# Attention and feed-forward layer: value products by head pair over 512 queries, three buffers of transposed probabilities, output blocks of two pairs

## The chip, the cores and the metric

The kernel runs on one core of one Trainium2 chip. The metric is the device time of one execution in microseconds, as the median of the runs shown. A profile is one further execution with its own time.

## The reference, cut to what matters

All tensors are float32: `x` is (8, 512, 256), there are 16 heads of 64, and the feed-forward part has 1024 hidden columns.

```python
def attn(x, gamma, w_qkv, w_out):            # called on layernorm(x)
    xn = rms_norm(x, gamma)
    q, k, v = split_heads(xn @ w_qkv)        # each (8, 16, 512, 64)
    sim = (q * 64**-0.5) @ k.transpose
    out = softmax(sim) @ v                   # (8, 16, 512, 64)
    return merge_heads(out) @ w_out

x = x + attn(layernorm(x), gamma, w_qkv, w_out)
x = x + ffn(layernorm(x), router_w, w1, b1, w2, b2)
# ffn: gelu(x @ w1 + b1) @ w2 + b2, times the sum of the two normalised top router weights
```

## The kernel before, in words

Every large product is computed from operands split in a high and a low fp32r part. The projections, the scores and the output projection take three products per tile (high·high, low·high, high·low, `products`, line 551); the products with the values take the high and the low part of the transposed probabilities against one set of values (`weighted_values`, line 617), whose high and low parts stand side by side in 128 stationary columns.

The attention is a pipeline of steps written out by hand. A head pair has four tiles n of 128 queries, so the 64 pairs give 256 tiles (`NUNIT`), and a step handles two: step s computes the scores of tiles 2s and 2s+1, and transposes the probabilities of tiles 2s-3 and 2s-2. Each engine runs its own list of work in a fixed order (the loops at lines 779, 914, 1020 and 1249), and semaphores join the lists. TensorE in step s does, in this order: transposes of tile 2s-3 into PSUM banks 4 and 5, scores of 2s and 2s+1 (banks 0 to 3), transposes of 2s-2 into banks 6 and 7, the auxiliary blocks of place 1, the products with the values of half t = s-2 (256 queries, both heads, bank 5), and the other auxiliary blocks.

An auxiliary block is one PSUM bank of other work: the query and key projections of the next pair (`q` in bank 4 and `k` in bank 6, on even steps), value projections of four heads (`v`, bank 4, on odd steps), and a tile of the output projection (`out`, bank 6, on odd steps). `plan_aux` (line 82) decides which block goes to which step and place; the place gives the bank (`PS_AUX`). An `out` block sums four pairs for one tile of 128 tokens (256 columns), and VectorE adds it to the residual `xres` (`aux_done`, line 1112); to keep four pairs and more, the attention output has `NATT` = 7 buffers.

The banks 4 to 7 are used in turn by transposes, by auxiliary blocks and by the value products, so a transpose waits until VectorE and ScalarE have emptied what stood there (`transpose_prob`, line 587). VectorE in step s does: reciprocal of the row sums of 2s-1 (L1189), the late auxiliary blocks of step s-1 (place above 1, among them `k` and `out`), low part of the transposed tile 2s-3 in two instructions (L1100), row maximum of 2s (L1184), low part of 2s-2, row maximum of 2s+1, reciprocal for 2s, the auxiliary blocks of place 1 (`q` or `v`), and last the layer norm work of a later input. ScalarE makes the high parts (L875 and L872), the exponentials (L882) and the copy of the value products to `halves_out` (L892). SyncE regroups that copy by DMA (`regroup`, line 439), and GpSimd normalises the probabilities (L974) and adds and splits the regrouped output (`attention_out`, line 1003).

The feed-forward part follows over eight inputs; its first products (`up`) lie in the last two attention steps, and its hidden values reuse the buffers `pT`.

Of the kernel before, what the change touches and what calls it, by code (L numbers as in the profile page):

```python
# [27 lines left out]
ALU = mybir.AluOpType  # L28
# [41 lines left out]
PS_OUT = 5  # L70
PS_AUX = {1: 4, 2: 6, 3: 7, 4: 5, 5: 4, 6: 5}
# [10 lines left out]
def plan_aux():  # L82
# [3 lines left out]
    for step in range(FIRST_STEP, LAST_STEP + 1):  # L86
        blocks = []
        if step == -4:
            blocks += [(2, "xt", 0), (3, "xt", 1)]
        if step == -3:  # L90
            blocks += [(1, "k", 0), (2, "q", 0)]
        if step == 0:
            blocks += [(5, "v", 0, 0), (6, "v", 0, 1)]
        if step % 2 == 0 and step // 2 + 1 in range(1, NPAIR):
            blocks += [(1, "q", step // 2 + 1), (2 if step else 4, "k", step // 2 + 1)]
        place = 2 if step < 11 else 1
        if step % 4 == 3 and (step + 1) // 4 in range(1, NPAIR // 2):
            blocks.append((place, "v", (step + 1) // 4, 0))
        if step % 4 == 1 and step // 4 in range(1, NPAIR // 2):
            blocks.append((place, "v", step // 4, 1))  # L100
# [11 lines left out]
    for tile in range(TT):  # L112
        task = ("out", 2 * B - 1, tile)
        index[task] = len(index)
        last_out.append((index[task], 0, *task))
# [3 lines left out]
def layer_kernel(nc, x, gamma_cols, w_qkv, w_out, router_w, w1, b1_cols, w2, b2_rows, ident, out):  # L119
# [11 lines left out]
    with ExitStack() as ctx:  # L131
# [39 lines left out]
        pT = [sb("pT_hi", [P, 2, 2 * TT, 2 * P], F32R), sb("pT_lo", [P, 2, 2 * TT, 2 * P], F32R)]  # L171
# [4 lines left out]
        halves_out = sb("halves_out", [P, 2, 2, 2 * P], F32, att)  # L176
# [17 lines left out]
        f_hT = [p[:, :, :, :].rearrange("p a k q -> p (a k q)").rearrange("p (f q) -> p f q", f=FT) for p in pT]  # L194
# [210 lines left out]
        def odd_tiles(n):  # L405

            t, u = divmod(n, 2)
            return [[p[:, t % 2, :, u * P + r * DH:u * P + (r + 1) * DH] for p in pT] for r in range(2)]

        def even_tile(n):  # L410
            t, u = divmod(n, 2)
            return [p[:, t % 2, :, u * P:(u + 1) * P].rearrange("p a (r q) -> p a r q", r=2) for p in pT]
# [12 lines left out]
        def _(sp):  # L425
# [13 lines left out]
            def regroup(pair):  # L439

                sp.wait_ge(s_halves, 2 * pair + 2)
                if pair >= 1:
                    sp.wait_ge(s_att, pair)
                for dst, rows, src_rows, h in ((att_hi_v, 0, 0, 0), (att_hi_v, DH, DH, 1),
                                               (att_lo_v, 0, DH, 0), (att_lo_v, DH, 0, 1)):
                    sp.dma_start(dst[rows:rows + DH, :].rearrange("p (a q) -> p a q", a=2),
                                 halves_out[src_rows:src_rows + DH, :, h, :]).then_inc(s_merge, 16)
# [23 lines left out]
            for slot in range(FIRST_SLOT, LAST_SLOT + 1):  # L471
# [21 lines left out]
                if rel == 19 and 1 <= b < B:  # L493
                    sp.wait_ge(s_aux, aux_index[("out", 2 * b - 1, TT - 1)] + 1)
                    sp.dma_start(x1_dram[b - 1], xres[:, :, :]).then_inc(s_x1, 16)
                if rel == 20 and 0 <= b < B:
                    if b >= 1:
                        sp.wait_ge(s_x1, 16 * b)
                    sp.dma_start(xres[:, :, :], x_v[b]).then_inc(s_xres, 16)
                    store_blocks(b + 1)  # L500
# [27 lines left out]
            sp.wait_ge(s_aux, aux_index[("out", 2 * B - 1, TT - 1)] + 1)  # L528
# [21 lines left out]
        def _(pe):  # L550
# [36 lines left out]
            def transpose_prob(n):  # L587
# [4 lines left out]
                before_rest = [block for block in before_rest if block[1] < 4]  # L592
                if n == 1:
                    pe.wait_ge(s_aux, aux_index[("v", 0, 1)] + 1)
                if n % 2:
# [21 lines left out]
            def weighted_values(t):  # L617

                pair = t // 2
                quad = pair // 2  # L620
                pe.wait_ge(s_ptlo, 4 * t + 4)
                pe.wait_ge(s_aux, aux_index[("v", quad, 1)] + 1)
                for h in range(2):
                    for part in range(2):
                        for k in range(TT):
                            ins = pe.matmul(ps[:, PS_OUT, h * 2 * P:(h + 1) * 2 * P],  # L626
                                            vbuf[:, quad % 2, k, pair % 2 * 2 + h, :],
                                            pT[part][:, t % 2, h * TT + k, :], start=part == 0 and k == 0,
                                            stop=part == 1 and k == TT - 1)
                ins.then_inc(s_pv, 1)  # L630
# [17 lines left out]
            def aux(step, block_no, place, kind, *args):  # L648

                tile = 2 * step - 3 if place == 1 else 2 * step - 2  # L650
                same_bank = [j + 1 for j in range(block_no) if aux_bank(j) == aux_bank(block_no)]
                if place and 0 <= tile < NUNIT:
# [42 lines left out]
                elif kind == "out":  # L695
                    half, tile = args
                    wait_weight_split(pe, 7)
                    for j in range(4):
                        pair = 4 * half + j
                        if tile == 0:  # L700
                            pe.wait_ge(s_att, pair + 1)
                        ins = products(bank[:, 0:D],
                                       [a[:, pair % NATT, tile * P:(tile + 1) * P] for a in attT],
                                       [w[:, pair % PAIRS, :] for w in wout], j == 0, j == 3)
# [3 lines left out]
            def last_outs():  # L708
# [6 lines left out]
                for j in range(4):  # L715
                    pair = NPAIR - 4 + j
                    pe.wait_ge(s_att, pair + 1)
                    for block_no, _, _, _, tile in last_out:
                        ins = products(ps[:, aux_bank(block_no), 0:D],
                                       [a[:, pair % NATT, tile * P:(tile + 1) * P] for a in attT],  # L720
                                       [w[:, pair % PAIRS, :] for w in wout], j == 0, j == 3)
                        if j == 3:
# [36 lines left out]
            def down(c, tile):  # L759
# [3 lines left out]
                for f in range(FT):  # L763
                    if tile == 0:
                        pe.wait_ge(s_hlo, c * FT + f + 1)
                    ins = products(ps[:, down_bank(c, tile), t * D:(t + 1) * D],
                                   [h[:, f, tile * P:(tile + 1) * P] for h in f_hT],
# [11 lines left out]
            for step in range(FIRST_STEP, LAST_STEP + 1):  # L779
# [16 lines left out]
                if 0 <= step - 2 < STEPS:  # L796
                    weighted_values(step - 2)
# [28 lines left out]
        def _(act):  # L826
# [39 lines left out]
            def transposed_hi(n):  # L866
                t = n // 2
                act.wait_ge(s_pt, 2 * n + 2)
                if n % 2 == 0:
                    if t >= 2:  # L870
                        act.wait_ge(s_pv, t - 1)
# [15 lines left out]
            def copy_halves(t):  # L887
                pair, part = divmod(t, 2)
                act.wait_ge(s_pv, t + 1)
                if part == 0 and pair >= 1:  # L890
                    act.wait_ge(s_merge, 64 * pair)
                act.activation(halves_out[:, part, :, :],  # L892
                               ps[:, PS_OUT, :].rearrange("p (h q) -> p h q", h=2), ACT.Copy).then_inc(s_halves, 1)
# [20 lines left out]
            for step in range(FIRST_STEP, LAST_STEP + 1):  # L914
# [5 lines left out]
                if step == 1:  # L920
                    exp(3)
                if 0 <= 2 * step - 3 < NUNIT:
# [12 lines left out]
                if 0 <= step - 2 < STEPS:  # L935
                    copy_halves(step - 2)
# [7 lines left out]


# [18 lines left out]
        def _(pool):  # L964
# [11 lines left out]
            def hidden_hi(n):  # L976
                c, f = divmod(n, FT)
                pool.wait_ge(s_gelu, n + 1)
                if c == 0 and f in (0, TT):
                    pool.wait_ge(s_pv, NHEAD - 1 + f // TT)  # L980
                if c >= 1 and f == 0:
                    pool.wait_ge(s_down, 2 * c)
                pool.tensor_scalar(f_hT[0][:, f, :], f_h[n % 3], 1.0, 1.0, ALU.mult, ALU.mult)\  # L983
# [19 lines left out]
            def attention_out(pair):  # L1003
# [3 lines left out]
                if pair >= NATT:  # L1007
                    pool.wait_ge(s_aux, aux_index[("out", (pair - NATT) // 4, TT - 1)] + 1)
# [400 lines left out]
```

## Time and profile before

| | |
|---|---|
| median of 3 runs | 1178.37 us (1178.27 to 1178.46) |
| the profiled execution's own time | 1178.86 us |
| its span, first to last instruction | 1177.0 us |
| TensorE matmul busy | 1164.9 us (99%) |
| VectorE busy | 977.3 us (83%) |
| ScalarE busy | 872.2 us (74%) |
| GpSimd busy | 665.6 us (57%) |

Busy time counts the instructions of an engine; TensorE's matmuls are pipelined, so that one matmul's span overlaps the next one's. The distance from one matmul's start to the next one's start is what it costs in a stream. In the timelines, PE is TensorE's matmul, PEld its weight load, DVE VectorE, ACT ScalarE, POOL GpSimd. The transposes of a tile (L612) begin a step: from one start of an odd tile's transposes to the next is the length of a step.

### The profile page before, as it was taken

How to read it: one execution, taken by the hardware profiler on the slowest of the kernel's cores; microseconds unless marked ns; L12 is line 12 of the kernel's file. 1: busy time of each engine (PE TensorE's matmuls, PEld its weight loads, DVE VectorE, ACT ScalarE, POOL GpSimd, SP SyncE). 2: the span in 40 equal slices, each digit the busy share in tenths (PEclk: the TensorE clock that was granted, in tenths of full speed). 3: DMA queues.
4: the chain of work that ended last, by engine and by line, in shares of the span. 5: the costliest groups of instructions: out<-in, count | busy, mean ns of one | idle time of the engine just before them, and what ended most of it. 6: DMA issues, size and time to landing. Idle time of an engine off the chain costs nothing.

```text
span 1177.0 us, 28904 instructions
## 1 busy us (share of the span) xinstructions
PE 1164.9 (99%) x11195; PEld 1024.8 (87%) x11195; DVE 977.3 (83%) x1736; ACT 872.2 (74%) x1897; POOL 665.6 (57%) x826
## 2 busy tenths in 40 slices
PE   8999999999999999999999999999999999999999
PEld 6778888888888888888888888888888887998898
DVE  6888888888888888889888988898889888877764
ACT  6888888888888888888888888888888885334432
POOL 5776565655556655656565656565656576223321
PEclk9999999999999999999999999999999999999999
DMA  4234111411141114111421132113211335334321
GB/s 125 61 88 109 33 32 33 123 37 38 37 127 37 38 37 126 37 38 37 117 47 37 38 92 69 33 33 85 72 38 37 91 90 150 127 111 145 109 74 36
DMA packets 74663, 83.08 MB, mean 71 GB/s; under 512 B 12576, under 2 KB 67360, under 8 KB 74528
## 3 DMA queue, kind: packets, MB, share of 16 engines
q1 hardware_dynamic: 74528, 81.24, 25.8%
q8 instruction: 89, 1.46, 0.5%
q14 instruction: 46, 0.38, 0.1%
HBM read 31.14 MB, written 16.25 MB: 40 GB/s over the span
## 4 chain that ended last, share of the span: by engine, by line
PE 86%; POOL 4%; DVE 2%; issue 2%; ACT 2%; POOLq 0%; DVEq 0%; ACTq 0%
PE ps L555 43%; PE ps L626 18%; PE ps L612 11%; PE ps L578 9%; PE ps L584 4%; POOL prob L974 1%; DVE pT_lo L1100 1%; ACT prob L882 1%; DVE negmax L1184 1%; POOL att_hi_v L1005 1%; POOL attT_lo L1011 1%; PE ps L741 1%; POOL wout_lo L995 0%; POOL attT_hi L974 0%; POOL wbig_lo L995 0%
## 5 line engine op out<-in xcount | busy, mean ns | idle before, releaser
L974 POOL TENSOR_SCALAR prob<-prob,rowinv 128x512 f32<-128x512 f32 x512 | 353.1, 704 | 241.5 <-DVE rowinv L1189 240.3
L882 ACT ACTIVATE prob<-ps,negmax 128x512 f32<-128x512 f32 x512 | 346.6, 685 | 34.6 <-DVE negmax L1184 30.6
L1100 DVE TENSOR_TENSOR pT_lo<-ps,pT_hi 128x512 fp32r<-128x512 f32 (+1 forms) x384 | 319.8, 860 | 19.9 <-ACT pT_hi L875 14.9
L1184 DVE TENSOR_REDUCE negmax<-ps 128x2 f32<-128x1024 f32 x256 | 310.2, 1212 | 1.4 <-PE ps L584 1.4
L872 ACT ACTIVATE pT_hi<-ps 128x1024 fp32r<-128x1024 f32 x128 | 131.4, 1027 | 101.1 <-issue 100.4
L612 PEld LDWEIGHTS ps<-identity,prob 64*128 64x128 f32 x4096 | 154.8, 138 | 58.2 <-issue 20.4
L612 PE MATMUL ps<-identity,prob 64*128 64x64 f32 x4096 | 177.9, 226 | 2.5 <-DVE vbuf L1100 1.1
L578 PE MATMUL ps<-nat 64*128 64x512 f32 x1024 | 171.0, 411 | 0.3 <-DVE nat L1101 0.3
L626 PE MATMUL ps<-pT_hi,vbuf 128*128 128x256 f32 x1024 | 164.7, 283 | 1.3 <-DVE pT_lo L1100 1.2
L626 PE MATMUL ps<-pT_lo,vbuf 128*128 128x256 f32 x1024 | 164.5, 283 | 0.0
L626 PEld LDWEIGHTS ps<-pT_hi,vbuf 128*128 128x128 f32 x1024 | 145.0, 191 | 7.4 <-DVE pT_lo L1100 2.0
L875 ACT ACTIVATE pT_hi<-ps 128x512 fp32r<-128x512 f32 x256 | 140.1, 608 | 10.4 <-PE ps L612 10.4
L626 PEld LDWEIGHTS ps<-pT_lo,vbuf 128*128 128x128 f32 x1024 | 141.2, 192 | 0.0
L1005 POOL TENSOR_TENSOR att_hi_v<-att_hi_v,att_lo_v 128x512 f32<-128x512 f32 x64 | 83.4, 1303 | 97.3 <-DMA att_lo_v<-halves_out 97.3
L555 PE MATMUL ps<-xT_hi,wbig_hi 128*128 128x512 f32 x316 | 131.4, 416 | 0.1
L555 PE MATMUL ps<-xT_hi,wbig_lo 128*128 128x512 f32 x316 | 124.5, 394 | 0.0
L555 PE MATMUL ps<-xT_lo,wbig_hi 128*128 128x512 f32 x316 | 123.0, 389 | 0.0
L1189 DVE RECIPROCAL rowinv<-rowsum 128x2 f32<-128x2 f32 x256 | 40.6, 159 | 92.9 <-ACT prob L882 92.6
L882 ACT ACTIVATION_READ_ACCUMULATOR prob<-ps,negmax 128x1 f32 x512 | 102.7, 201 | 0.0
L983 POOL TENSOR_SCALAR pT_hi<-prob 128x512 fp32r<-128x512 f32 x64 | 50.6, 795 | 90.8 <-ACT prob L899 90.8
L584 PE MATMUL ps<-nat 64*128 64x512 f32 x512 | 101.7, 394 | 0.0
L578 PEld LDWEIGHTS ps<-nat 64*128 64x128 f32 x1024 | 87.4, 188 | 12.9 <-DVE nat L1101 0.7
(114 smaller groups left out, 2292.4 us busy)
## 6 DMA issues: line engine op xcount, KB each, us to landing
att_hi_v<-halves_out SPq DMA_DIRECT2D x128, 128.0 KB, 2.3
att_lo_v<-halves_out SPq DMA_DIRECT2D x128, 128.0 KB, 2.4
blocks_scratch<-xblocks SPq DMA_DIRECT2D x15, 512.0 KB, 5.1
xn<-blocks_scratch SPq DMA_DIRECT2D x60, 128.0 KB, 2.8
xin<-in_x SPq DMA_DIRECT2D x32, 128.0 KB, 3.2
xres<-in_x SPq DMA_DIRECT2D x8, 512.0 KB, 4.3
x_scratch<-xres SPq DMA_DIRECT2D x8, 512.0 KB, 3.6
xin<-x_scratch SPq DMA_DIRECT2D x32, 128.0 KB, 3.2
```

What stands on the lines that cost most here:

```text
L555: ins = pe.matmul(dst, stationary[i], moving[j], start=first and n == 0, stop=last and n == len(terms) - 1)
L578: pe.matmul(ps[:, PS_SCORE[n % 2] + h, :], part[rows, q_part, q0:q0 + P], part[rows, k_part, :], start=q_part == QH, stop=False)
L584: pe.matmul(ps[:, PS_SCORE[n % 2] + h, :], part[rows, QH, q0:q0 + P], part[rows, KL, :], start=False, stop=True).then_inc(s_score, 1)
L612: ins = pe.transpose(ps[:, bank + r, a * DH:(a + 1) * DH], prob[rows, n % NPROB, a * P:(a + 1) * P], identity[rows, rows])
L626: ins = pe.matmul(ps[:, PS_OUT, h * 2 * P:(h + 1) * 2 * P], vbuf[:, quad % 2, k, pair % 2 * 2 + h, :], pT[part][:, t % 2, h * TT + k, :], ...
L872: act.activation(even_tile(n)[0], two_bank_blocks(PS_PT_EVEN), ACT.Copy).then_inc(s_pthi, 2)
L875: act.activation(odd_tiles(n)[r][0], bank_blocks(PS_PT_ODD + r), ACT.Copy).then_inc(s_pthi, 1)
L882: act.activation(prob[:, n % NPROB, j * SEQ:(j + 1) * SEQ], ps[:, PS_SCORE[n % 2] + j, :], ACT.Exp, bias=negmax[:, n % 4, j:j + 1], accum_ ...
L974: return pool.tensor_scalar(dst, src, scalar, 1.0, ALU.mult, ALU.mult)
L1005: pool.tensor_tensor(att_hi_v[:, :], att_hi_v[:, :], att_lo_v[:, :], ALU.add).then_inc(s_head, 1)
L1100: return dve.tensor_tensor(dst, full, hi, ALU.subtract)
L1184: dve.tensor_reduce(negmax[:, n % 4, :], ps[:, PS_SCORE[n % 2]:PS_SCORE[n % 2] + 2, :], AX.X, ALU.max, negate=True).then_inc(s_max, 1)
```

## The change

The products with the values are issued once for a pair instead of once for half of its queries: on every odd step, each of the two heads gets its own bank (5 and 6) and a matmul has 512 moving columns. For this `pT` has three buffers of 256 queries. When a pair's two halves lie in buffers 2 and 0, the buffers are read in the order 0, 2, and the tokens of that pair are permuted (`pair_tokens`). An `out` block sums two pairs instead of four, for two tiles of 128 tokens (512 columns of a bank), on every even step, in bank 5; `attT` has three buffers instead of seven. `q`, `v` and `out` are now in the first group of a step (place 1 or 2), `k` alone is late (place 3, bank 6). ScalarE copies one head at a time: head 0 within the odd step, head 1 at the start of the next step. GpSimd's `attention_out` moves behind the normalisation of tile 2s. The copy of `xres` in and out of memory moves to earlier slots; the last output blocks sum two pairs instead of four, and VectorE adds them before the last two hidden values.

```diff
-PS_OUT = 5
-PS_AUX = {1: 4, 2: 6, 3: 7, 4: 5, 5: 4, 6: 5}
+PS_VALUES = (5, 6)
+PS_AUX = {1: 4, 2: 5, 3: 6, 4: 5, 5: 4, 6: 5, 7: 6, 8: 7}
@@ plan_aux
-            blocks += [(1, "q", step // 2 + 1), (2 if step else 4, "k", step // 2 + 1)]
-        place = 2 if step < 11 else 1
+            blocks += [(1, "q", step // 2 + 1), (3 if step else 4, "k", step // 2 + 1)]
...
-        for half in range(2 * B - 1):
-            since = step - (8 * half + 11)
-            steps = (0, 2, 3, 4) if half == 2 * B - 2 else (0, 2, 4, 6)
-            if since in steps:
-                blocks.append((2, "out", half, steps.index(since)))
+        for quarter in range(NPAIR // 2 - 1):
+            since = step - (4 * quarter + 8)
+            if quarter == NPAIR // 2 - 2 and since == 0:
+                blocks += [(1, "out", quarter, 0), (2, "out", quarter, 1)]
+            elif quarter < NPAIR // 2 - 2 and since in (0, 2):
+                blocks.append((2, "out", quarter, since // 2))
@@ buffers
+        NHALF = 3
+        pT = [sb("pT_hi", [P, NHALF, 2 * TT, 2 * P], F32R), sb("pT_lo", [P, NHALF, 2 * TT, 2 * P], F32R)]
-        NATT = 7
+        NATT = 3
@@ aux_of: which blocks of a step are first, which late
-            return [block for block in blocks if block[1] == 1], [block for block in blocks if block[1] > 1]
+            return [block for block in blocks if block[1] <= 2], [block for block in blocks if block[1] > 2]
+        def pair_at(step):
+            pair, odd = divmod(step - 3, 2)
+            return pair if not odd and 0 <= pair < NPAIR else None
@@ regroup
-                sp.wait_ge(s_halves, 2 * pair + 2)
...
+                for h, dst in ((0, (att_hi_v, att_lo_v)), (1, (att_lo_v, att_hi_v))):
+                    sp.wait_ge(s_halves, 2 * pair + h + 1)
...
@@ transpose_prob
+                valued = pair_at(step - 1)
                 if n % 2:
                     if before_first:
                         pe.wait_ge(s_aux, before_first[-1][0] + 1)
                     elif n >= 2:
                         pe.wait_ge(s_ptlo, 2 * (n - 2) + 2)
-                    if step >= 3:
-                        pe.wait_ge(s_halves, step - 2)
+                    if valued is not None:
+                        pe.wait_ge(s_halves, 2 * valued + 1)
                 else:
...
+                    if valued is not None:
+                        pe.wait_ge(s_halves, 2 * valued + 2)
@@ weighted_values
-                pe.wait_ge(s_ptlo, 4 * t + 4)
                 for h in range(2):
+                    pe.wait_ge(s_ptlo, 2 * min(TT * pair + TT + h, NUNIT))
                     for part in range(2):
                         for k in range(TT):
-                            ins = pe.matmul(ps[:, PS_OUT, h * 2 * P:(h + 1) * 2 * P], ...
-                                            pT[part][:, t % 2, h * TT + k, :], ...
+                            ins = pe.matmul(ps[:, PS_VALUES[h], :], ...
+                                            pT[part][:, halves_of(pair)[0], h * TT + k, :], ...
@@ aux, kind "out"
+                    quarter, part = args
+                    for i in range(2):
+                        for pair in (2 * quarter, 2 * quarter + 1):
+                            ins = products(bank[:, i * D:(i + 1) * D],
+                                           [a[:, pair % NATT, pair_tokens(pair, 2 * part + i)] for a in attT],
+                                           [w[:, pair % PAIRS, :] for w in wout], pair % 2 == 0, pair % 2 == 1)
@@ ScalarE's loop
+                if pair_at(step - 1) is not None:
+                    copy_halves(pair_at(step - 1), 1)
                 if 0 <= 2 * step - 3 < NUNIT:
                     transposed_hi(2 * step - 3)
...
-                if 0 <= step - 2 < STEPS:
-                    copy_halves(step - 2)
+                if pair_at(step) is not None and step < LAST_STEP:
+                    copy_halves(pair_at(step), 0)
@@ GpSimd's loop
-                if step % 2 == 0 and 0 <= step // 2 - 2 < NPAIR:
-                    attention_out(step // 2 - 2)
...
                     normalise_prob(2 * step)
+                if pair_at(step - 1) is not None:
+                    attention_out(pair_at(step - 1))
@@ VectorE, aux_done, kind "out"
-                    dve.tensor_tensor(xres[:, tile, :], bank[:, 0:D], xres[:, tile, :], ALU.add)\
-                        .then_inc(s_aux, 1)
+                    tiles = slice(2 * part, 2 * part + 2)
+                    dve.tensor_tensor(xres[:, tiles, :], bank.rearrange("p (t d) -> p t d", t=2), xres[:, tiles, :],
+                                      ALU.add).then_inc(s_aux, 1)
@@ VectorE, feed-forward loop, first input
+                    if f == FT - 3 and c == 0:
+                        for block_of_out in last_out:
+                            aux_done(*block_of_out)
                 if c == 0:
-                    for block_of_out in last_out:
-                        aux_done(*block_of_out)
```

## Rows read from the trace of the kernel before

**Rows 1.** The page: busy times, the clock in 40 slices.

```profile
PE 1164.9 (99%) x11195; PEld 1024.8 (87%) x11195; DVE 977.3 (83%) x1736; ACT 872.2 (74%) x1897; POOL 665.6 (57%) x826
...
PEclk9999999999999999999999999999999999999999
```

**Rows 2.** Timeline of TensorE, an even step: start, us, line, operation, tiles.

```profile
401.00 0.71 PE L612 MATMUL ps<-identity,prob 64*128 64x64 f32 x16
...
403.57 0.50 PE L555 MATMUL ps<-xT_hi,wbig_hi 128*128 128x512 f32 x1
...
405.07 0.64 PE L626 MATMUL ps<-pT_hi,vbuf 128*128 128x256 f32 x4
...
406.98 0.40 PE L555 MATMUL ps<-xT_hi,wbig_hi 128*128 128x512 f32 x1
...
408.14 0.39 PE L555 MATMUL ps<-xT_lo,wbig_hi 128*128 128x512 f32 x1
```

**Rows 3.** The same timeline, the odd step behind it.

```profile
408.46 0.71 PE L612 MATMUL ps<-identity,prob 64*128 64x64 f32 x16
...
412.59 0.64 PE L626 MATMUL ps<-pT_hi,vbuf 128*128 128x256 f32 x4
...
414.51 0.28 PE L555 MATMUL ps<-wout_hi,attT_hi 128*128 128x256 f32 x1
...
416.04 0.71 PE L612 MATMUL ps<-identity,prob 64*128 64x64 f32 x16
```

**Rows 4.** Timeline of VectorE in the even step.

```profile
402.41 1.29 DVE L1100 TENSOR_TENSOR pT_lo<-ps,pT_hi 128x512 fp32r<-128x512 f32 x2 [0.27 <-ACT pT_hi L875]
...
404.89 1.22 DVE L1100 TENSOR_TENSOR pT_lo<-ps,pT_hi 128x1024 fp32r<-128x1024 f32 x1
...
407.16 0.15 DVE L1189 RECIPROCAL rowinv<-rowsum 128x2 f32<-128x2 f32 x1
407.23 0.67 DVE L1101 SCALAR_TENSOR_TENSOR nat<-ps,nat 128x512 fp32r<-128x512 f32 x1
407.82 0.41 DVE L1076 BATCH_NORM_STATS2 ln_stats<-xin 128x6 f32<-128x256 f32 x1
```

**Rows 5.** Groups by line and shape: VectorE subtracts and adds with a PSUM operand.

```profile
L1100 DVE TENSOR_TENSOR nat<-ps,nat 128x512 fp32r<-128x512 f32 x64 | 44.2, 691 | 21.0 <-ACT nat L851 21.0
L1112 DVE TENSOR_TENSOR xres<-ps,xres 128x256 f32<-128x256 f32 x64 | 26.6, 418 | 1.4 <-PE ps L555 1.2 <-issue 0.3
```

**Rows 6.** Timelines of VectorE and TensorE at 24 us: transposes that wait for VectorE.

```profile
23.63 0.75 DVE L1100 TENSOR_TENSOR vbuf<-ps,vbuf 128x256 fp32r<-128x256 f32 x2 [0.34 <-ACT vbuf L857]
...
24.43 0.71 PE L612 MATMUL ps<-identity,prob 64*128 64x64 f32 x16 [0.65 <-DVE vbuf L1100]
```

**Rows 7.** Timeline of ScalarE: copy of the value products, exponential, key tile, the next step.

```profile
407.18 0.60 ACT L892 ACTIVATE halves_out<-ps 128x512 f32<-128x512 f32 x1 [0.38 <-PE ps L626]
407.67 0.68 ACT L882 ACTIVATE prob<-ps,negmax 128x512 f32<-128x512 f32 x1
...
409.00 0.60 ACT L851 ACTIVATE nat<-ps 128x512 fp32r<-128x512 f32 x1
```

**Rows 8.** Timeline of GpSimd: the output of a pair added and split.

```profile
404.64 1.29 POOL L1005 TENSOR_TENSOR att_hi_v<-att_hi_v,att_lo_v 128x512 f32<-128x512 f32 x1 [1.39 <-DMA att_lo_v<-halves_out]
...
406.73 1.30 POOL L1011 TENSOR_TENSOR attT_lo<-att_hi_v,attT_hi 128x512 fp32r<-128x512 f32 x1
```

**Rows 9.** Timeline of TensorE: first transposes of steps 8 and 126, first down product.

```profile
68.47 0.71 PE L612 MATMUL ps<-identity,prob 64*128 64x64 f32 x16
...
958.65 0.71 PE L612 MATMUL ps<-identity,prob 64*128 64x64 f32 x16
...
1000.03 0.36 PE L555 MATMUL ps<-wbig_hi,pT_hi 128*128 128x256 f32 x1 [1.70 <-issue]
```

**Rows 10.** Timelines of ScalarE and GpSimd: the last pair's copy and last split.

```profile
984.95 0.60 ACT L892 ACTIVATE halves_out<-ps 128x512 f32<-128x512 f32 x1 [2.21 <-PE ps L626]
...
994.36 1.29 POOL L1011 TENSOR_TENSOR attT_lo<-att_hi_v,attT_hi 128x512 fp32r<-128x512 f32 x1
```

More of the change, by code:

```diff
@@ L112, in plan_aux @@
     for tile in range(TT):
-        task = ("out", 2 * B - 1, tile)
+        task = ("out", NPAIR // 2 - 1, tile)
         index[task] = len(index)
@@ L193, in layer_kernel, with hidden @@
         f_h = [prob[:, 1, 0:SEQ], prob[:, 1, SEQ:2 * SEQ], prob[:, 0, 0:SEQ]]
-        f_hT = [p[:, :, :, :].rearrange("p a k q -> p (a k q)").rearrange("p (f q) -> p f q", f=FT) for p in pT]
+        def hidden(part, f):
+            assert (STEPS - 2) % NHALF == 0
+            place = 2 * (f % TT)
+            return pT[part][:, 0 if f >= TT else 2, place:place + 2, :].rearrange("p k q -> p (k q)")
         ffn = ctx.enter_context(ExitStack())
@@ L439, in regroup @@
             def regroup(pair):
-                sp.wait_ge(s_halves, 2 * pair + 2)
                 if pair >= 1:
                     sp.wait_ge(s_att, pair)
[L444 to L447, printed above, removed]
+                for h, dst in ((0, (att_hi_v, att_lo_v)), (1, (att_lo_v, att_hi_v))):
+                    sp.wait_ge(s_halves, 2 * pair + h + 1)
+                    for part in range(2):
+                        sp.dma_start(dst[part][h * DH:(h + 1) * DH, :],
+                                     halves_out[part * DH:(part + 1) * DH, h, :]).then_inc(s_merge, 16)
             def load_input(m):
@@ L695, in aux @@
                 elif kind == "out":
[L696 to L704, printed above, removed]
+                    quarter, part = args
+                    wait_weight_split(pe, 6 if quarter < 2 else 7)
+                    if part == 0:
+                        pe.wait_ge(s_att, 2 * quarter + 2)
+                    for i in range(2):
[3 more added lines that the diff above has]
+                                           [w[:, pair % PAIRS, :] for w in wout], pair % 2 == 0, pair % 2 == 1)
                 ins.then_inc(s_auxfull, 1)
@@ L714, in last_outs @@
                         pe.wait_ge(s_aux, same_bank[-1])
-                for j in range(4):
-                    pair = NPAIR - 4 + j
+                for pair in (NPAIR - 2, NPAIR - 1):
                     pe.wait_ge(s_att, pair + 1)
@@ L719, in last_outs @@
                         ins = products(ps[:, aux_bank(block_no), 0:D],
-                                       [a[:, pair % NATT, tile * P:(tile + 1) * P] for a in attT],
-                                       [w[:, pair % PAIRS, :] for w in wout], j == 0, j == 3)
-                        if j == 3:
+                                       [a[:, pair % NATT, pair_tokens(pair, tile)] for a in attT],
+                                       [w[:, pair % PAIRS, :] for w in wout], pair % 2 == 0, pair % 2 == 1)
+                        if pair == NPAIR - 1:
                             ins.then_inc(s_auxfull, 1)
@@ L766, in down @@
                     ins = products(ps[:, down_bank(c, tile), t * D:(t + 1) * D],
-                                   [h[:, f, tile * P:(tile + 1) * P] for h in f_hT],
+                                   [hidden(i, f)[:, tile * P:(tile + 1) * P] for i in range(2)],
                                    [w[:, f, :] for w in w2s], f == 0, f == FT - 1)
@@ L795, in _ @@
                     up(0, tail + 1)
-                if 0 <= step - 2 < STEPS:
-                    weighted_values(step - 2)
+                if pair_at(step) is not None:
+                    weighted_values(pair_at(step))
                 for block_of_aux in rest:
@@ L943, in _ @@
                 split_weights(2 * step + 1)
+            copy_halves(NPAIR - 1, 0)
+            copy_halves(NPAIR - 1, 1)
             def router_exp(c):
```

85 lines of the change are left out of this document (46 added, 39 removed).

## Prediction

> **What bounds the kernel now.** I read the page first. TensorE is busy 99% of the span and its clock is granted in full in every slice, VectorE follows with 83% [rows 1]. A share of 99% says that TensorE sets the end now; it doesn't say how much room the others have behind it, and this change shifts work between the steps. So the second view is the timeline of one pair of steps on TensorE, and the third the same stretch on VectorE.
>
> An even step runs from 401.00 to 408.46, 7.46 us; the odd one behind it to 416.04, 7.58 us; together 15.04 [rows 2, 3]. In the even step the transposes and scores take 2.57, `q` 1.50 (to 405.07), the value products 1.91 (to 406.98), `k` with the turn to the next transposes 1.48. In the odd step 4.13 pass before the values start, they take 1.92, and `out` with its turn 1.53. No matmul in these rows waits.
>
> VectorE works in a loop with TensorE. Its first low part of the even step starts at 402.41, that is 1.41 after the odd tile's transposes, because ScalarE must make the high part first; from there it goes almost without pause through low part, row maximum, low part, row maximum, reciprocal and the low part of `q`, which ends at 407.90 (407.23 + 0.67) [rows 4]. The next transposes need the `q` bank empty. They come at 7.46, the bank is free at 6.90: the room in an even step is 0.56 us. That is the number on which this change turns.
>
> **The change, part by part.**
>
> *Value products.* 32 matmuls of 256 columns per pair become 16 of 512. The first cost 1.91 per 16 [rows 2], 0.1195 each. A 512-column matmul with 128 stationary columns is in the trace: from 406.98 to 408.14 there are five distances in `k`, 0.232 each [rows 2]. Per pair 32 x 0.1195 - 16 x 0.232 = 0.11 us less; 64 pairs, 7 us. The turn from the last matmul of `k` to the transposes is 408.46 - 408.14 - 0.232 = 0.09.
>
> The Trainium skill ("TensorE: Matmul & The Clock Gate", Part 1) gives the start-to-start distance of warm matmuls as columns over 2.4 GHz plus about 2.5 ns. The trace doesn't agree: it has 0.232 us at 512 columns where the page's form gives 0.216. By the page 16 such matmuls would take 3.45 us and not 3.71, and the sum below would come out some 15 us lower; I stay with the row.
>
> *Length of the steps if nothing waits.* Odd: 4.13 + 16 x 0.232 + 0.09 = 7.93. Even: 2.57 + 1.50 for `q`, `out` 1.53 - 0.09 = 1.44, `k` 1.48: 6.99. Together 14.92 against 15.04. So the even step gets shorter by 0.47 and the odd longer by 0.35.
>
> *`out` moves into the first group and into bank 5.* It lies between `q` and `k` on TensorE, and on VectorE its add stands behind the low part of `q`. The transposes of the next odd tile write banks 4 and 5, and their wait now names the last block of the first group: the add of `out`. Before, the add of `out` was late work of an odd step, for bank 6, of which the transposes come second. What does the add cost? An add of 256 columns from PSUM takes 0.42 and a subtract of 512 columns 0.69 [rows 5]; the new one has 512 columns and the form of the second. Bounds: 0.42 below, and twice the first, 0.84, above; I take 0.70.
>
> VectorE in the even step, from the transposes' start: chain as before until the next instruction can start behind `q` at 407.82, which is 6.82 [rows 4]; the matmuls of `out` are done by 5.6 (2.57 + 1.50 + 1.44 and their drain), so the add starts at 6.82 and ends at 7.52. The transposes at 24.43 started 0.05 after the VectorE instruction that they waited for (23.63 + 0.75 = 24.38) [rows 6]. So the next odd tile's transposes start at 7.57 and not at 6.99: a stall of 0.58 us on TensorE. It can't be filled by running ahead: the chain starts with those transposes' own predecessor (1.41), and everything between is in order on VectorE. With the bounds of the add the even step is 7.29 to 7.71.
>
> Queued behind the waiting transposes are the scores and the transposes of the even tile, and behind these VectorE's next chain; the loop closes through them, so the stall is paid in full in each period. Period: 7.57 + 7.93 = 15.50 against 15.04. The adds also double in number of columns (60 blocks of 512 against 60 of 256), which is why VectorE doesn't get this back elsewhere.
>
> *The other waits of the odd step.* Here the room is large: the low part of `v` stands in the chain where `q` does in the even step, so it ends about 7.0, and TensorE comes at 7.93. The copy of head 0 can start when its products are done, about 6.2; copy and exponential follow (0.60, then two exponentials, 1.33 from 407.67 to 409.00) [rows 7], the copy of head 1 begins about 8.05 and ends about 0.65 into the even step, before ScalarE needs to start the high part at 0.77 (the 1.41 less a high part of 0.60 and the turn of 0.04). It is close: nothing to 0.1 us per pair; I take nothing. Layer norm work stands behind the add on even steps and can push the next low part from 1.41 to 1.9, which the odd step's room of 0.9 swallows.
>
> *`attention_out` behind the normalisation.* It takes 3.4 us (404.64 to 408.03) [rows 8] and starts in the even step at about 7.7, so the normalisation of tile 2s+1 ends about 12.5 after the even step's start. TensorE transposes this tile at 15.5. Nothing. The new waits on `attT` (three buffers) are for `out` blocks that TensorE has finished 3 us before. Regrouping by head has 3 us of room before GpSimd asks. The round trip of `xres` has over 5 us of room. Nothing for any of the three; if one of them were late, the price is TensorE's wait for `out` in a few steps, 1 us each.
>
> *Start.* Steps 2 to 7 took 68.47 - 24.43 = 44.04 [rows 6, 9]. New: even steps without `out` are set by `q`, 6.95; odd ones 7.93; three of each, 44.6. Plus 0.6.
>
> *End.* Step 126 has neither `q` nor values now and is 7.0 long by the chain with 4.0 of work. The last pair's two heads come together, 1.8 us later than the last half did. From the last copy's start to the last split's end 10.7 us pass (984.95 to 995.65) [rows 10]; TensorE covers this with the last `out` blocks of three pairs before, of one pair now, 2.9 less, and waits some 1.5. On the other side regrouping by head takes two DMA issues off that path, and the 1.70 idle before the first down product [rows 9] goes, because the adds of the last blocks come earlier. Bounds: 3 less to 4 more; I take 0, the difference of these terms.
>
> *Sum.* Steps 8 to 125, 59 pairs: before 958.65 - 68.47 = 890.2 [rows 9], after 59 x 15.50 = 914.5, plus 24.3. A few odd spots lengthen the pairs before to a mean of 15.09; I let half of it stand, plus 1.4. With the start 0.6: 1178.86 + 26 = 1205 us. The profiled execution lies 0.5 above the median of the runs; by that the median would be 1204.5, and I say 1205.
>
> **Rivals.**
>
> *A. The add is hidden and the value products gain.* It would be so if the next transposes did not have to wait for the add, or the chain on VectorE could start earlier. Then 59 x 0.12 to 0.17 come back: 1170 to 1173, faster. For it: before the change no such wait shows on TensorE's rows, and all the edits except one are at no cost. Against it: the room is 0.56 us minus the 0.47 by which the even step shrinks, 0.09 us, and the add is at least 0.42. It decides at an add of 0.12 us. Chance 8%.
>
> *B. The stall spreads.* ScalarE has one copy more before the high part at the start of the even step. If the exponential of the odd step ends later than 8.05, the high part, the whole VectorE chain and so the next transposes move with it. The margin is 0.1 us. The price is what the copy shifts, up to its 0.60: 59 x 0.3 on the average makes 1223, at most 1240. For it: the copy waits for TensorE already before (0.38 idle) [rows 7]. Against it: the odd step has become longer by 0.35, which gives ScalarE time. Chance 7%.
>
> *C. The add is shorter or lies partly beside other work.* With 0.42 the even step is 7.29 and the time 1189. Chance 5%; it lies just below the range.
>
> **How the numbers follow.** Forecast, the stall of 0.58 in each of 59 pairs: 80%. A 8%, B 7%, C 5%. The time of the likeliest is 1205. Its own range, from the ends of the add near its value (0.65 to 0.75), the copy's 0 to 0.1, the end's 3 less to 4 more and the odd spots: 1197 to 1213. For 8 in 10 I keep 1195 to 1214. What can be told from no change here is about 0.2%, 2.4 us. Faster: A where the 0.11 of each pair arrives, 6%. Same: A where the start, the end and the copy eat it up, 2%. Slower: forecast, B and C, 92%.
>
> **What would show it.** In the profile after: the wait list has TensorE's transposes released by VectorE's add to `xres`, some 59 times, about 0.6 us each; the distance between the starts of odd tiles' transposes alternates 7.57 and 7.93; 512-column matmuls in the value products 0.232 apart; the add 0.70 long; TensorE's busy share down to about 96%. The prediction is wrong if that wait is absent or a tenth of this, if the odd step is the one with the wait, or if the value products run at another distance.

## The result, and the profile after

The changed kernel takes 1209.72 us (median of 4 runs, 1208.83 to 1210.07) against 1178.36 before: ratio 1.0263, 95% interval 1.025 to 1.0275. It is slower by 31 us. Its profiled execution has a span of 1207.0 us, 30.0 more than before.

The page first: busy times and the clock. TensorE is busy 96% where it was 99% [rows 1], and the chain that ended last now runs to a third over VectorE.

```profile
PE 1158.2 (96%) x10171; PEld 964.5 (80%) x10171; DVE 1006.8 (83%) x1738; ACT 879.2 (73%) x1897; POOL 664.4 (55%) x826
...
PEclk9999999999999999999999999999999999999999
...
PE 57%; DVE 33%; ACT 4%; issue 4%; POOL 1%; DMA 1%; SPq 0%; DVEq 0%; POOLq 0%; ACTq 0%
```

There are 1024 matmuls fewer. In 40 slices the clock looks as before; a short fall near the end does not show in them (below). The list of waits (engine and line that waited, for whom, us in total, times, longest) names one that was not there:

```profile
PE ps L639 <- DVE xres L1144: 32.9, 60, 2.7
```

Sixty waits of TensorE's transposes for VectorE's add to the residual. The timeline of TensorE in an even step and the odd one behind it shows where it stands (start, us, engine, line, operation, tiles, idle before and releaser):

```profile
456.72 0.71 PE L639 MATMUL ps<-identity,prob 64*128 64x64 f32 x16
```

```profile
464.29 0.71 PE L639 MATMUL ps<-identity,prob 64*128 64x64 f32 x16 [0.51 <-DVE xres L1144]
...
468.40 1.09 PE L652 MATMUL ps<-pT_hi,vbuf 128*128 128x512 f32 x4
469.33 1.07 PE L652 MATMUL ps<-pT_lo,vbuf 128*128 128x512 f32 x4
470.24 1.07 PE L652 MATMUL ps<-pT_hi,vbuf 128*128 128x512 f32 x4
471.15 1.07 PE L652 MATMUL ps<-pT_lo,vbuf 128*128 128x512 f32 x4
472.15 0.71 PE L639 MATMUL ps<-identity,prob 64*128 64x64 f32 x16
```

The even step lasts 464.29 - 456.72 = 7.57 us, the odd one 7.86, together 15.43 against 15.04 [rows 2, 3]. Four value products take 0.91 to 0.93, 0.23 each. Fifty-nine of the sixty even steps, 8 to 124, have the same form (step 126, with the wait of 2.7, comes below); VectorE's timeline in the one that ends at 417.28:

```profile
411.13 1.29 DVE L1127 TENSOR_TENSOR pT_lo<-ps,pT_hi 128x512 fp32r<-128x512 f32 x2 [0.99 <-ACT pT_hi L899]
...
415.96 0.67 DVE L1128 SCALAR_TENSOR_TENSOR nat<-ps,nat 128x512 fp32r<-128x512 f32 x1
416.55 0.68 DVE L1144 TENSOR_TENSOR xres<-ps,xres 128x512 f32<-128x512 f32 x1
```

and the transposes it releases, behind TensorE's last matmul of `k`:

```profile
416.38 0.39 PE L579 MATMUL ps<-xT_lo,wbig_hi 128*128 128x512 f32 x1
417.28 0.71 PE L639 MATMUL ps<-identity,prob 64*128 64x64 f32 x16 [0.51 <-DVE xres L1144]
```

The chain from the low part to `q`'s end is that of [rows 4]; the add follows at once and ends at 417.23; the transposes start 0.05 later, as in [rows 6]. The list counts 0.51 of idle time per wait, since it starts at the end of the last matmul's own 0.39; without the wait the transposes would have come 0.32 behind that matmul's start, as before (0.232 and the turn of 0.09), and they come 0.90 behind it: 0.58 lost.

Where the 30.0 us are: up to step 8, 0.4 (steps 2 to 7 take 68.85 - 24.21 = 44.64 against 44.04, and they begin 0.2 earlier); steps 8 to 125, 25.3 (984.28 - 68.85 = 915.4 against 890.2); from step 126 to the first down product 3.5 (1029.20 - 984.28 = 44.9 against 41.4 [rows 9]); the rest 0.8.

In that end the clock falls once. TensorE idled 2.71 us up to 993.13; from 994.3 to 997.7 its granted clock is 0.5, the lower level of 1.2 GHz, and then full again. The kernel before has no such stretch up to its last microsecond. Two groups of instructions in the fall:

```profile
994.53 1.07 PE L602 MATMUL ps<-nat 64*128 64x512 f32 x4
...
996.81 1.59 PE L652 MATMUL ps<-pT_hi,vbuf 128*128 128x512 f32 x4
```

At full clock such groups take 0.62 and 1.09. At half clock 3.4 us hold 1.7 us of work; that is the most that this fall can have cost. A slice of the page is 30 us long, so that its digit stays 9. Two runs below give a price: in e5 the same wait of 2.70 has no fall behind it, and from step 127 to the first down product it takes 35.46 us against 36.07, though another wait there is 0.50 longer; e6 has a second such fall later and takes 37.28. By these numbers one fall costs 1.1 to 1.2 us, an estimate.

### The profile page after: what moved, and what is told of

Same layout as the page of the kernel before. It is cut to its first block, busy times and chain, and to the rows that moved or that the text cites. A ratio compares the mean times of both kernels' runs of the same rounds, so it can differ in the third digit from the quotient of the medians.

```text
span 1207.0 us, 26802 instructions
## 1 busy us (share of the span) xinstructions
PE 1158.2 (96%) x10171; PEld 964.5 (80%) x10171; DVE 1006.8 (83%) x1738; ACT 879.2 (73%) x1897; POOL 664.4 (55%) x826
## 4 chain that ended last, share of the span: by engine, by line
PE 57%; DVE 33%; ACT 4%; issue 4%; POOL 1%; DMA 1%; SPq 0%; DVEq 0%; POOLq 0%; ACTq 0%
PE ps L579 22%; PE ps L652 18%; DVE pT_lo L1127 13%; DVE negmax L1216 10%; PE ps L639 9%; PE ps L602 4%; ACT pT_hi L899 3%; DVE nat L1128 3%; DVE xres L1144 3%; PE ps L608 2%; DVE xn L1123 1%; DVE rowinv L1221 1%; DVE nat L1127 1%; PE ps L765 0%; POOL prob L1001 0%
## 5 line engine op out<-in xcount | busy, mean ns | idle before, releaser
L639 PE MATMUL ps<-identity,prob 64*128 64x64 f32 x4096 | 177.3, 226 | 37.6 <-DVE xres L1144 32.9
L652 PE MATMUL ps<-pT_hi,vbuf 128*128 128x512 f32 x512 | 139.0, 393 | 0.1
L652 PE MATMUL ps<-pT_lo,vbuf 128*128 128x512 f32 x512 | 137.1, 389 | 0.0
L652 PEld LDWEIGHTS ps<-pT_lo,vbuf 128*128 128x128 f32 x512 | 96.1, 188 | 20.7
L652 PEld LDWEIGHTS ps<-pT_hi,vbuf 128*128 128x128 f32 x512 | 92.4, 190 | 16.4 <-DVE pT_lo L1127 0.5
L915 ACT ACTIVATE halves_out<-ps 128x512 f32<-128x512 f32 x128 | 77.2, 603 | 14.0 <-PE ps L652 14.0
L1038 POOL TENSOR_TENSOR attT_lo<-att_hi_v,attT_hi 128x512 fp32r<-128x512 f32 x64 | 82.4, 1287 | 5.3
```

Source lines behind the costliest of these rows:

```text
L639: ins = pe.transpose(ps[:, bank + r, a * DH:(a + 1) * DH], prob[rows, n % NPROB, a * P:(a + 1) * P], identity[rows, rows])
L652: ins = pe.matmul(ps[:, PS_VALUES[h], :], vbuf[:, quad % 2, k, pair % 2 * 2 + h, :], pT[part][:, halves_of(pair)[0], h * TT + k, :], start ...
L1038: pool.tensor_tensor(attT[1][:, pair % NATT, :], att_hi_v[:, :], attT[0][:, pair % NATT, :], ALU.subtract).then_inc(s_att, 1)
```

## The experiments

All edits are made to the changed kernel unless said otherwise, and are shown shortened. Times are medians; before stood at 1178.0 to 1178.6 beside them.

### e1: the add cut to 64 columns

```diff
-dve.tensor_tensor(xres[:, tiles, :], bank..., xres[:, tiles, :], ALU.add)
+dve.tensor_tensor(xres[:, tiles, 0:32], bank...[:, :, 0:32], xres[:, tiles, 0:32], ALU.add)
```

> The kernel after, with the add of an output block cut from 512 to 64 columns; the rest of the sum is left out. Theory (the add stands between an odd tile's transposes and their bank): an add of 64 columns is about 0.23 us (0.68 at 512 and 0.42 at 256 give 1.0 ns per column), so the even step ends at 6.82 + 0.23 + 0.05 = 7.10 instead of 7.57 us; 60 steps, 28 us less: about 1182. Rival (the copy of head 1 on ScalarE and the load of the engines as a whole set the period): VectorE is relieved, but the step stays near 7.57: above 1200.

Measured: 1182.83 (1182.31 to 1183.88), ratio to before 1.0043 (1.0029 to 1.0057); 27 us below the changed kernel. The add took 0.21, the even step 7.10. The group of the add (count | busy, mean ns):

```profile
L1144 DVE TENSOR_TENSOR xres<-ps,xres 128x64 f32<-128x64 f32 x62 | 13.2, 213 | 1.1 <-PE ps L579 1.1
```

The theory's 7.10 and 1182 are met. From 0.68 to 0.21 is 0.47 in the add and 0.47 in the step. The kernel leaves out seven eighths of each add, so its output is not the layer's.

### e4: the add done twice

```diff
+if quarter or part: dve.wait_ge(s_aux, ...)      # VectorE's own previous add
+dve.tensor_tensor(spare[:, :, :], bank..., xres[:, tiles, :], ALU.add)
 dve.tensor_tensor(xres[:, tiles, :], bank..., xres[:, tiles, :], ALU.add)
```

> The kernel after, with the add of each output block done twice, once into a spare buffer. Theory: the whole of the second add, about 0.60 us back to back, is paid in each of 60 even steps: 36 us more, 1246; the even step becomes 8.17. Rival (part of the add is beside other work): less than half of that, under 1228.

Measured: 1243.81 (2 runs), 34 us above the changed kernel, and the even step is 8.16. The wait doubled:

```profile
PE ps L640 <- DVE xres L1149: 68.7, 60, 3.3
```

It rose from 32.9 to 68.7 over 60 waits, 0.60 each: the whole of the second add. With e1 the step is a straight line in the add's length from 0.21 to 1.28 us.

### e6: the add ahead of `q`

```diff
-for block_of_aux in aux_of(step)[0]:
+for block_of_aux in aux_of(step)[0][::-1] if 8 <= step <= 126 else aux_of(step)[0]:
     aux_done(*block_of_aux)
```

> The kernel after, with the order of the low part of q and the add of the output block exchanged on VectorE. Theory (what counts is the sum of what VectorE must do between two odd transposes, not which instruction is last): no difference, 1208 to 1211, and the wait is put down to q instead of the residual. Rival (the add as such is what is waited for, and q could hide behind it): about 0.6 us less in each even step, 1175.

Measured: 1209.77 (2 runs), the changed kernel's time. The same wait has another name:

```profile
PE ps L639 <- DVE nat L1128: 30.2, 59, 0.5
```

The step is 7.57 as before. The releaser in a wait list is whoever comes last in the queue. What is waited for is the sum of what VectorE has to do between two odd tiles' transposes.

### e5: the copy of head 1 done twice

```diff
+if h == 1 and pair < NPAIR - 1:
+    act.activation(spare[:, :], ps[:, PS_VALUES[h], :], ACT.Copy)
 act.activation(halves_out[:, h, :], ps[:, PS_VALUES[h], :], ACT.Copy).then_inc(s_halves, 1)
```

> The kernel after, with the copy of head 1 at the start of an even step done twice on ScalarE, once into a spare buffer. Theory (the loop from an odd tile's transposes to the next goes through ScalarE's high part, and the copy ends just before it): the second copy, 0.5 us back to back, pushes the high part by about 0.45, and the even step grows by as much: 63 steps, 28 us more, 1238. Rival (ScalarE has room there): under 1215.

Measured: 1219.29 (2 runs), 10 us above the changed kernel and not 28. ScalarE's timeline at the start of an even step in this kernel:

```profile
507.26 0.69 ACT L907 ACTIVATE prob<-ps,negmax 128x512 f32<-128x512 f32 x1
507.83 0.21 ACT L907 ACTIVATION_READ_ACCUMULATOR prob<-ps,negmax 128x1 f32 x1
507.93 0.60 ACT L917 ACTIVATE spare<-ps 128x512 f32<-128x512 f32 x1
```

The even step that starts at 492.24 ends at 499.95 with the next odd tile's transposes: 7.71 against 7.57, so 0.14 longer and not 0.45. The even step shown starts at 507.81, and its first copy 0.12 into it, behind the exponentials. In the one at 492.24 the two copies start at 492.35 and 492.84 and the high part at 493.32, which is 1.08 into the step where the changed kernel has 0.78: 0.30 later. VectorE's low part moves by as much, from 1.41 to 1.72, and VectorE recovers half of this on the way to its add. The forecast of 0.45 was three times too high. Neither theory's number was met. That a second copy costs 0.14 does not yet say what the first one costs; this is read from the start of the low part, which stands 1.41 into the even step in the kernel before and 1.41 in the changed one. So ScalarE's copy is no second cause of the loss.

### e2: the value products in 256 columns

```diff
-for part in range(2): for k in range(TT):
-    pe.matmul(ps[:, PS_VALUES[h], :], ..., pT[part][:, halves_of(pair)[0], ...])
+for i in range(2): for part in range(2): for k in range(TT):
+    pe.matmul(ps[:, PS_VALUES[h], i * 2 * P:(i + 1) * 2 * P], ..., pT[part][:, (2 * pair + ...) % NHALF, ...])
```

> The kernel after, each value product of 512 columns issued as two of 256 into the same bank. Theory: the odd step is set by TensorE, so the whole difference shows: 32 x 0.1195 - 16 x 0.2275 = 0.18 us per pair, 64 pairs, 12 us more: about 1221. Rival (the wide products bring nothing because the odd step also ends on another engine): no difference, 1210.

Measured: 1220.38 (1220.2 to 1220.95), 10.7 us above the changed kernel. The odd step went from 7.86 to 8.04, the even one stayed at 7.57. The wide products do bring what they were worth, 0.18 per pair; the gain lies in the step that TensorE sets.

### e7: GpSimd's `attention_out` put back ahead of the normalisation

> The kernel after, with GpSimd's attention_out put back ahead of the normalisation of tile 2s. Theory (the move costs and brings nothing while TensorE is held by the add): 1207 to 1213, with the body of the attention unchanged. Rival (the late output of a pair is part of the loss): 1200 or less.

Measured: 1204.24 (2 runs, 1203.37 and 1205.11), 5.5 below the changed kernel. Neither theory. The changed kernel has in each of seven inputs two odd steps that are longer, 8.13 and 8.30 instead of 7.86. In e7 twelve of these fourteen are back within 0.05 of 7.86, the other two are 8.00 and 7.98, and six other odd steps are now 7.93 to 8.38; steps 8 to 125 are 3.4 us shorter in all. VectorE and GpSimd in the changed kernel, in the odd step from 417.28:

```profile
418.01 0.77 DVE L1110 TENSOR_SCALAR ln_var<-ln_mv 128x4 f32<-128x4 f32 x1
418.70 0.15 DVE L1221 RECIPROCAL rowinv<-rowsum 128x2 f32<-128x2 f32 x1
418.77 0.67 DVE L1127 TENSOR_TENSOR nat<-ps,nat 128x512 fp32r<-128x512 f32 x1
```

```profile
417.46 1.29 POOL L1032 TENSOR_TENSOR att_hi_v<-att_hi_v,att_lo_v 128x512 f32<-128x512 f32 x1
418.85 0.62 POOL L1001 TENSOR_SCALAR attT_hi<-att_hi_v 128x512 fp32r<-128x512 f32 x1
```

and the same instruction on VectorE in e7, beside GpSimd's shorter scalings (`prob`, 0.7 each) and not beside an addition:

```profile
417.70 0.20 DVE L1110 TENSOR_SCALAR ln_var<-ln_mv 128x4 f32<-128x4 f32 x1
```

Four elements per partition took 0.77 instead of 0.20 and ended at 418.78, with GpSimd's addition (418.75). This is so in all seven inputs of the changed kernel: 0.77 or 0.78, ending 0.02 to 0.03 behind the addition. In e7 the seven are 0.17 to 0.66, and the long ones end with a scaling. e1 shows it from the other side: there the instruction starts 0.06 to 0.07 into the addition, takes 1.25 or 1.26, and the one long odd step per input is 8.60 to 8.63; 0.48 more in the instruction, 0.48 more in the step. Two steps on, the layer norm's `xn` (L1123) does the same in the changed kernel: 1.80 for two where 1.11 is usual, the last ending at 434.65, 0.15 behind GpSimd's addition (1.25 in e7). The late `k` part behind them makes the even tile's transposes wait. The Trainium skill says ("SBUF — State Buffer", SBUF: two separate sides) that VectorE and GpSimd share one port pair as an exclusive lock, and that a VectorE instruction in a two-port mode blocks for the whole of a GpSimd instruction that came first. The ends agree with it, 0.57 us more for an instruction of 0.20; in which mode this instruction ran, no row says. So the move of `attention_out` was not free: it laid long additions beside VectorE's layer norm instructions.

The move also lengthened step 126, which is 8.85 in the changed kernel and 6.97 in e7. This gain did not last in the profiled execution of e7: from step 127 to the first down product it takes 37.97 us against 36.07, with two stretches at 1.2 GHz, behind idle times of 2.51 and 1.94, where the changed kernel has one. The two profiled executions are 3.7 us apart.

### e3: ScalarE copies the block, GpSimd adds it

```diff
+act.activation(out_copy[:, :, :], ps[:, aux_bank(block_no), :]..., ACT.Copy).then_inc(s_outcopy, 1)   # behind q's high part
+pool.tensor_tensor(xres[:, tiles, :], out_copy[:, :, :], xres[:, tiles, :], ALU.add).then_inc(s_outadd, 1)   # one step later
@@ transpose_prob
-pe.wait_ge(s_aux, before_first[-1][0] + 1)
+pe.wait_ge(s_aux, upto(before_first[-1][0]))            # q alone
+pe.wait_ge(s_outcopy, moved_upto(before_first[-1][0]))  # the copy
```

> The kernel after, but the output block is copied from PSUM by ScalarE, in the gap before its second exponential, and GpSimd adds the copy to the residual one step later. Theory: the next transposes wait for the low part of q (6.90) and for the copy (about 6.4), neither later than TensorE's own work, so the even step is 6.99 and the odd one 7.86: 14.85 against 15.43, 60 pairs, 35 us less, and the wait of 2.7 us in step 126 goes too: 1172 to 1175, below the kernel before. Rival (the stall is the load of the whole pipeline, or ScalarE's copy moves the exponential): the period stays above 15.04 and the time above 1180.

Measured: 1181.63 (1180.26 to 1184.17), ratio to before 1.0034 (1.0022 to 1.0047): 28 us below the changed kernel, but not below the kernel before and not at the theory's 1172 to 1175. The period is the theory's way and the time the rival's. TensorE in a pair of steps (starts of the odd tiles' transposes):

```profile
398.04 0.72 PE L657 MATMUL ps<-identity,prob 64*128 64x64 f32 x16
...
405.03 0.71 PE L657 MATMUL ps<-identity,prob 64*128 64x64 f32 x16
...
412.96 0.71 PE L657 MATMUL ps<-identity,prob 64*128 64x64 f32 x16
```

6.99 and 7.93: no wait is left in a pair, and 14.92 is 0.12 below the 15.04 of before. The even step is the theory's, the odd one is 0.07 longer than its 7.86. Steps 8 to 125 take 885.5 against 890.2. The end took it back, 48.6 us from step 126 to the first down product against 41.4. The two longest waits of TensorE in steps 126 to 128 are for probabilities that come through GpSimd, and for a low part of VectorE that waits for ScalarE, where the weights' high part and two copies of value products stand in the queue:

```profile
959.20 1.05 PE L657 MATMUL ps<-identity,prob 64*128 64x64 f32 x16 [2.23 <-POOL prob L1025]
...
974.45 1.20 PE L657 MATMUL ps<-identity,prob 64*128 64x64 f32 x16 [2.23 <-DVE pT_lo L1163]
```

### e8: the same, with the end relieved

```diff
 def moved(task):
-    return task[0] == "out" and task[1] < NPAIR // 2 - 2
+    return task[0] == "out" and task[1] < NPAIR // 2 - 3
-slot_of_chunks.update({NUNIT - 7: [8], NUNIT - 2: [9]})
+slot_of_chunks.update({NUNIT - 5: [8], NUNIT - 2: [9]})
```

> The kernel with the block copied by ScalarE and added by GpSimd, in which the last quarter before the end (steps 124 and 126) stays on VectorE and the split of the first feed-forward weights on GpSimd moves from step 124 to step 125. Theory (the body gained 4.7 us against the kernel before, 885.5 for steps 8 to 125 against 890.2, and the end lost 7 through GpSimd, which splits weights, adds and turns the next input in the same two steps): GpSimd's delays of 2.2 us at the end go, 4 to 6 us less: 1175 to 1178, just below the kernel before. Rival (the end is bound by the last pair's longer value products and the smaller cover): no gain, 1181.

Measured: 1177.85 (11 runs, 1175.85 to 1181.31), ratio to before 0.9994 (0.9985 to 1.0003). 3.8 us less than e3, in the expected range, but no difference from the kernel before can be told. Left at the end are TensorE's waits

```profile
961.28 0.71 PE L657 MATMUL ps<-identity,prob 64*128 64x64 f32 x16 [2.52 <-DVE xres L1185]
...
993.75 0.39 PE L595 MATMUL ps<-wout_hi,attT_hi 128*128 128x256 f32 x1 [1.94 <-POOL attT_lo L1062]
```

of which the second is the rival's: the last pair, with less work to cover it. Behind it the granted clock is 0.5 from about 994.4 to 997.8.

### e9: e8 with `attention_out` ahead of the normalisation

The edit of e7 on e8.

> The kernel e8 (ScalarE copies the block, GpSimd adds it, later split) with attention_out back ahead of the normalisation of tile 2s, which took 5 us off the changed kernel in e7. Theory (what that order cost there was VectorE's layer norm instructions held up by GpSimd's long ones beside the late even step, and in e8 those have 0.1 us of room): the normalisation of 2s now ends about 8.9 after the even step's start and TensorE transposes the tile at 9.0, so nothing is lost, the layer norm steps of 7.19 become 6.99, 1 to 3 us less than e8: 1175 to 1177. Rival (the normalisation is late for the transposes): 0.1 to 0.3 us in each pair, 1184 to 1196.

Measured: 1197.87 (1193.79 to 1200.26), ratio 1.0157 (1.0141 to 1.0173), 20 us above e8. The rival is right, and its price of at most 1196 was still too low. The theory's part is there too: the even steps with layer norm work are nearly all back at 6.99, 3.2 us in all. Many pairs are still 6.99 and 7.94, but other odd steps are 8.2 to 9.8 and one is 11.8, and of this line e8's list has only one wait of 0.7:

```profile
PE ps L657 <- POOL prob L1025: 8.2, 11, 2.0
```

The list counts idle time only. The timeline of TensorE has nearly the whole loss, 22.8 us in the odd steps 9 to 125, at one place, the even tile's transposes. The time between the start of the last scores and theirs, 0.26 as a rule, is 13.8 us longer in all; the list has GpSimd's `prob` as the releaser eleven times and the late `k` seven times. The transposes themselves take 0.33 longer in each of 21 steps, 6.7 in all. A further 1.2 are in the step of 11.8: TensorE idled 1.99 up to 201.93, and from about 202.3 to 205.8 the granted clock is 0.5. So the same exchange in GpSimd's order saves 5 us in the changed kernel and costs 20 in the form without the add's wait.

## Why the prediction was right

1205 was forecast, 1209.7 measured, within the range of 1195 to 1214, slower as forecast.

*The stall.* The step of the argument that carried it, the room of 0.56 us in the even step against its shortening by 0.47 and an add behind it, held to 0.01: even step 7.57 forecast, 7.57 measured; add 0.70 against 0.68; release 0.05 against 0.05; 59 such waits, as forecast. The "about 0.6 us each" expected in the wait list stands there as 0.51, since the list starts at the end of the matmul before; the loss per step is 0.58. e1 and e4 moved the step by the add's length in both directions, e6 showed that it is the chain's sum, and e3 took the wait away and 28 us with it. Rival A is out: a faster kernel would have needed an add of 0.12.

*The value products.* 7 us was expected from them; e2 gives 10.7 for the width, since the products come 0.2275 to 0.232 apart and not all 0.232, and the odd step is 7.86 instead of 7.93 (0.02 in front of the products, the rest in them and in the turn). The Trainium skill's distance ("TensorE: Matmul & The Clock Gate", Part 1), 0.216 at 512 columns, isn't met by the value products either: four take 0.91 to 0.93.

*The sum of the body.* 914.5 and 1.4 forecast, 915.4 measured. This is better than its parts, and in so far luck: the odd step was forecast 0.07 too long, 4 us over 59 pairs, and against that stand 5 us that I had put at nothing.

*Two terms at nothing that were not.* "Layer norm work ... the odd step's room of 0.9 swallows" and the "Nothing" for `attention_out` behind the normalisation were wrong together. The room was counted for VectorE's chain, but the late part of `k` is waited for by the even tile's transposes after 2.0 us, not after 7.9; and GpSimd's additions made the layer norm instructions longer. Cost: 0.27 and 0.44 us once per input, 5 us over seven inputs. Of this e7 gives back 3.4 in steps 8 to 125.

*The end.* Forecast 0 with bounds of 3 less and 4 more, measured 3.5 more. The wait before the last pair is 1.95 (forecast 1.5) and the idle 1.70 before the first down product is gone as forecast. Missed were two things. One is step 126, 8.85 long and not 7.0: from 976.6 to 986.0 GpSimd adds a pair, splits weights and splits the next input, so that the even tile's probabilities come 0.98 late there, and the chain ends 2.71 after TensorE's work:

```profile
987.76 1.05 PE L639 MATMUL ps<-identity,prob 64*128 64x64 f32 x16 [0.98 <-POOL prob L1001]
...
993.13 0.72 PE L639 MATMUL ps<-identity,prob 64*128 64x64 f32 x16 [2.71 <-DVE xres L1144]
```

In e7, with the pair's addition back ahead of the normalisation, the step is 6.97: so this, too, is the move that was put at nothing. The other is the clock: the wait of 2.71 is followed by 3.4 us at 1.2 GHz, 1.1 to 1.2 us by the estimate above, for which the prediction has no term. The two make 3.0 of the end's 3.5, and the 3.5 are most of the distance between 1205 and 1209.7.

*Rival B* was given a margin of 0.1 us; e5 shows that 0.5 us more on ScalarE costs 0.14, so the mechanism exists and is mild; with one copy the low part starts at 1.41, not moved at all.

## What to carry to other kernels

When work moves between the stages of a hand-written pipeline, compare each stage's length on the bounding engine with the chain through the other engines between two uses of the same bank: 0.12 us was gained per pair on TensorE (e3), and 0.58 lost because the stage that became shorter was also the one that got a longer chain. A wait list names the last instruction of such a chain; changing their order changes the name, not the time. Engines with idle time, here ScalarE with 27% and GpSimd with 45%, can take over a link of the chain (e3), but then look at the few steps where they have their own extra work. And look at the clock in stretches of a microsecond where TensorE has idled for about 2 us: a fall of 3.4 us does not show in a page of 40 slices.

## What the runs showed of the hardware

A VectorE `tensor_scalar` of four elements per partition took 0.77 us instead of 0.17 to 0.20 beside a GpSimd addition from SBUF, and 1.25 where it started 0.06 to 0.07 behind the addition's start (e1); each time it ended with the addition. In e8 it starts 0.05 ahead of such an addition and takes 0.17. GpSimd's scalings of 0.7 do the same to it on a smaller scale (0.52 to 0.66 in four inputs of e7). The instructions that read PSUM kept their lengths (0.67 for `k` beside a scaling, 1.27 for two low parts beside an addition).

Value products of 512 columns come 0.2275 to 0.232 us apart and those of 256 columns 0.12 apart, so a matmul twice as wide costs 0.01 less than two.

TensorE's idle 0.51 to 0.58 us in every 15.4 left its clock granted in full (1.00 from 150 to 950 us). Single idle times of about 2 us and more were followed, at most 1.2 us after work had begun again, by some 3.4 us at 1.2 GHz: in the changed kernel behind 2.71, in e9 behind 1.99. It is not so each time: e5 has 2.70 at the same place and no fall, and the changed kernel's idle 1.95 at the end has none where e6 has one.
